# v as the stationary operand and probabilities divided before they are turned, in a two-layer attention and mixture-of-experts kernel

## What is computed

```python
q = (xn @ w_q).reshape(b, n, HEADS, DIM_HEAD).transpose(0, 2, 1, 3)
k, v = jnp.split(xn @ w_kv, 2, axis=-1)            # and the same for k and v
k = jnp.concatenate([nk, k], axis=2)               # 2 null keys in front of 256
v = jnp.concatenate([nv, v], axis=2)
sim = einsum(l2norm(q), l2norm(k)) * 8.0 + alibi, causal
out = softmax(sim) @ v
out = out.transpose(...).reshape(b, n, HEADS * DIM_HEAD) @ w_out
```

## Time and profile before

| | us |
|---|---|
| median of three timed executions | 655.25 (651.95 to 656.0) |
| the profiled execution, its own time | 660.73 |
| its span from first to last instruction | 658.9 |

### The profile page before, as it was taken

How to read it: one execution, slowest core, us unless ns; L and a number is a source line. 1 busy time by engine, 2 the same in 40 slices (tenths; PEclk the granted TensorE clock), 3 DMA queues, 4 the chain that set the end, 5 groups by cost and what they waited for, 6 DMA issues and landing times.

```text
span 658.9 us, 13422 instructions
## 1 busy us (share of the span) xinstructions
PE 573.4 (87%) x3792; PEld 453.3 (69%) x3792; DVE 421.6 (64%) x1523; ACT 430.3 (65%) x1197; POOL 356.6 (54%) x310
## 2 busy tenths in 40 slices
PE   2446979987899989888999999999999999998787
PEld 1444768875567767766777777777877777777566
DVE  5773836455688676889655665665656566577653
ACT  2712857535677787766577777767767776877562
POOL 3618845033888697444275544544455433688830
PEclk9999979999699999999999999999999999999899
DMA  9502223140110013000000000011001100111100
GB/s 317 197 4 53 70 68 74 49 152 16 27 32 25 18 33 97 1 1 2 1 24 23 25 22 23 27 29 21 21 27 29 25 14 10 29 48 49 53 21 9
DMA packets 26326, 29.13 MB, mean 44 GB/s; under 512 B 3920, under 2 KB 22384, under 8 KB 25744
## 3 DMA queue, kind: packets, MB, share of 16 engines
q1 hardware_dynamic: 21680, 18.89, 8.9%
q0 software_dynamic: 4576, 9.38, 6.2%
HBM read 19.94 MB, written 8.32 MB: 43 GB/s over the span
## 4 chain that ended last, share of the span: by engine, by line
PE 59%; DVE 15%; POOL 11%; issue 9%; ACT 3%; DMA 1%; another core or an unknown queue 1%; SPq 0%; POOLq 0%; DVEq 0%; ACTq 0%
PE b_last L1816 8%; PE b_upB L1801 7%; POOL taken L622 5%; PE b_rest L1865 4%; PE b_upB L1787 4%; PE b_last L1679 3%; POOL rn L571 3%; PE b_rest L1654 3%; PE b_rest L1613 2%; PE b_upA L1472 2%; PE b_upA L1734 2%; PE b_last L1472 2%; PE b_rest L1836 2%; PE b_upA L1474 2%; PE b_upA L1473 2%
## 5 line engine op out<-in xcount | busy, mean ns | idle before, releaser
L868 ACT ACTIVATE prb<-prb,mneg 128x130 f32<-128x130 f32 (+1 forms) x256 | 114.8, 450 | 93.9 <-DVE mneg L1415 89.4
L571 POOL TENSOR_TENSOR rn<-ss,halves 128x8 f32<-128x8 f32 x64 | 107.6, 1681 | 102.0 <-DVE ss L1353 101.3
L1415 DVE CUSTOM_DVE_ANT_0 prb<-b_upB,bias 128x130 f32<-128x130 f32 (+1 forms) x256 | 82.1, 356 | 122.1 <-PE b_upB L1801 117.5
L499 POOL DMA_INDIRECT moe_buf<-normal_rows,source x79 | 78.8, 997 | 103.1 <-PE b_rest L1768 63.5
L1816 PEld LDWEIGHTS b_last<-v,prT_all 128*128 128x128 f32 x768 | 100.0, 192 | 12.6 <-DVE qs_all L1401 4.8
L1816 PE MATMUL b_last<-v,prT_all 128*128 128x64 f32 x768 | 101.4, 268 | 3.0 <-DVE qs_all L1401 2.4
L1801 PE MATMUL b_upB<-qkT 64*128 64x258 f32 (+1 forms) x512 | 77.7, 381 | 0.0
L877 ACT ACTIVATE prT_all<-b_rest 128x512 f32<-128x512 f32 (+1 forms) x128 | 61.5, 480 | 10.9 <-PE b_rest L1865 7.8
L1865 PE MATMUL b_rest<-cst,prb 128*128 128x128 f32 x384 | 63.6, 275 | 0.0
L314 POOL TENSOR_TENSOR qk<-qk,rn 128x512 f32<-128x512 f32 x56 | 59.1, 1055 | 4.4
L1865 PEld LDWEIGHTS b_rest<-cst,prb 128*128 128x128 f32 x384 | 47.6, 150 | 18.0 <-issue 17.8
(11 more groups left out here) (325 smaller groups left out, 1294.2 us busy)
## 6 DMA issues: line engine op xcount, KB each, us to landing
expert_rows<-moe_buf SPq DMA_DIRECT2D x20, 128.0 KB
expert_rows<-moe_buf SPq DMA_DIRECT2D x39, 64.0 KB
bias<-w_up SPq DMA_DIRECT2D x1, 2048.0 KB, 8.9
down<-w_dn SPq DMA_DIRECT2D x2, 1024.0 KB, 10.0
moe_buf<-w_up SPq DMA_DIRECT2D x4, 512.0 KB, 3.9
moe_buf<-normal_rows,source POOLq DMA_INDIRECT x79
qk<-x SPq DMA_DIRECT2D x8, 128.0 KB, 4.0
v<-w_qk SPq DMA_DIRECT2D x1, 1024.0 KB, 11.5
```

What stands on the lines that cost most here:

```text
L499: nc.gpsimd.indirect_dma_start(out=room, out_offset=None, in_=normal_rows[layer], in_offset=bass.IndirectOffsetOnAxis(ap=source[layer][:, ...
L571: nc.gpsimd.tensor_tensor(rn[hs], ss[hs], halves[:], ALU.pow).then_inc(pool_root, 1)
L868: nc.scalar.activation(prb[k % 3][:, i, 0:n], prb[k % 3][:, i, 0:n], ACT.Exp, scale=-1.0, bias=mneg[:, qt, h:h + 1], accum_out=lsum[:, qt, ...
L1415: nc.vector.tensor_tensor_reduce(prb[k % 3][:, i, 0:n], b_sim[i][:, 0:n], bias[:, h, KEYS - n:KEYS], 1.0, FMAX, ALU.add, ALU.min, mneg[:, ...
```

## The change

Four things are changed together.

1. The values matmul is swapped: `v` (64 columns of one head) is stationary, `prT` (128 columns) moves. The output comes out with channels on the partitions, head 0 of a pair in partitions 0 to 63 and head 1 in 64 to 127 of `b_pv`, so the turn L1836 and the copy out of `b_y` are gone; one VectorE copy takes `b_pv` to `oT`. The built program puts these matmuls on array tiles of 128 rows by 64 columns, at column 0 for head 0 and column 64 for head 1.
2. The null values are swapped likewise: four float32r matmuls of 128 moving columns in place of one of 512.
3. Since the sums now run along the wrong axis for a division behind the matmul, the probabilities are divided while they still have a query on each partition: for every step VectorE takes two reciprocals and multiplies head 0, and head 1 is multiplied by ScalarE for k < 32 and by GpSimd from there on.
4. The division takes a turn of its own: turning, copying, null columns and values come one turn later. The first layer's row gathers on GpSimd are spread over turns.

```diff
@@ GpSimd
-                if s % 3 == 0 and 0 <= s < 3 * (B - 2):
-                    take_rows(s // 3 + 2)
+                for b in range(2, B):
+                    parts = [n for n in range(2 * T) if s == 3 * (b - 2) + 2 * n // 3]
+                    if parts:
+                        take_rows(b, parts)
...
+            def shares(s):
+                for k in [k for k in step_at(s, 1) if k >= ACT_SHARES]:
+                    qt, hp = divmod(k % STEPS, HP)
+                    n, h = NULL + P * (qt + 1), 2 * hp + 1
+                    pool.wait_ge(dve_rl, k + 1)
+                    pool.wait_ge(act_exp, 2 * k + 2)
+                    mine = prb[k % 3][:, 1, 0:n]
+                    nc.gpsimd.tensor_tensor(mine, mine, rl[:, qt, h:h + 1].to_broadcast([P, n]), ALU.mult).then_inc(pool_share, 1)
...
-            all_steps(rows, tile_rows, take_tiles, front)
+            all_steps(shares, rows, tile_rows, take_tiles, front)
@@ ScalarE
+            def shares(s):
+                for k in [k for k in step_at(s, 1) if k < ACT_SHARES]:
...
+                    nc.scalar.activation(prb[k % 3][:, 1, 0:n], prb[k % 3][:, 1, 0:n], ACT.Copy, scale=rl[:, qt, h:h + 1]).then_inc(act_share, 1)
...
-                for k in step_at(s, 1):
+                for k in step_at(s, 2):
@@ VectorE, scores(s)
-                for m in quad_at(s, 7):
...
-                    nc.vector.reciprocal(heads8, lsum[:, tile, first:first + HALF]).then_inc(dve_rl, 1)
...
-                    nc.vector.tensor_tensor(o_half[m % 2].rearrange("p (h d) -> p h d", h=HALF), b_pv.rearrange("p (h d) -> p h d", h=HALF),
-                                            heads8.unsqueeze(2).to_broadcast([P, HALF, DH1]), ALU.mult).then_inc(dve_norm, 1)
+                for m in quad_at(s, 8):
+
+                    dve.wait_ge(pe_pvn, m + 1)
+                    if m:
+                        dve.wait_ge(pe_op, m)
+                    nc.vector.tensor_copy(oT[:].rearrange("p a q -> p (a q)"), b_pv).then_inc(dve_oT, 1)
...
-                for m in quad_at(s, 5):
+                for k in step_at(s, 1):
+
+                    qt, hp = divmod(k % STEPS, HP)
+                    n, h = NULL + P * (qt + 1), 2 * hp
+                    dve.wait_ge(act_exp, 2 * k + 2)
+                    nc.vector.reciprocal(rl[:, qt, h:h + 2], lsum[:, qt, h:h + 2]).then_inc(dve_rl, 1)
+                    dve.wait_ge(dve_rl, k + 1)
+                    mine = prb[k % 3][:, 0, 0:n]
+                    nc.vector.tensor_scalar(mine, mine, rl[:, qt, h:h + 1], None, ALU.mult).then_inc(dve_share, 1)
+                for m in quad_at(s, 6):
...
-                for k in step_at(s, 1):
+                for k in step_at(s, 2):
...
-                    dve.wait_ge(act_exp, 2 * k + 2)
+                    dve.wait_ge(dve_share, k + 1)
+                    if k < ACT_SHARES:
+                        dve.wait_ge(act_share, k + 1)
+                    else:
+                        dve.wait_ge(pool_share, k + 1 - ACT_SHARES)
@@ TensorE
-                for k in step_at(s, 3):
+                for k in step_at(s, 4):
...
-                    for i in range(2):
-                        h = 2 * (p % HP) + i
-                        at = (k % 4 * 2 + i) * DH1
-                        for c in range(p // HP + 1):
-                            ins = nc.tensor.matmul(b_pv[:, at:at + DH1], prT[k % 3][:, i, c * P:(c + 1) * P], v[:, c, h * DH1:(h + 1) * DH1],
-                                                   start=(k % 4 == 0 and i == 0 and c == 0), stop=False, skip_group_check=True)
+                    at = k % 4 * P
+                    for c in range(p // HP + 1):
+                        for i in range(2):
+                            h = 2 * (p % HP) + i
+                            ins = nc.tensor.matmul(b_pv[i * DH1:(i + 1) * DH1, at:at + P], v[:, c, h * DH1:(h + 1) * DH1],
+                                                   prT[k % 3][:, i, c * P:(c + 1) * P], start=(k % 4 == 0 and c == 0), stop=False,
+                                                   skip_group_check=True)
...
-                    nc.tensor.matmul(b_pv, pnT[:], nvbd[:, m % 2], start=False, stop=True, skip_group_check=True).then_inc(pe_pvn, 1)
+                    for a in range(4):
+                        ins = nc.tensor.matmul(b_pv[:, a * P:(a + 1) * P], nvbd[:, m % 2, a * P:(a + 1) * P], pnT[:], start=False, stop=(a == 3),
+                                               skip_group_check=True)
...
-                    for i in range(4):
-                        ins = nc.tensor.transpose(b_y[:, i * P:(i + 1) * P], o_half[m % 2][:, i * P:(i + 1) * P], ident)
-                    ins.then_inc(pe_oT, 1)
...
-                    pe.wait_ge(act_exp, 2 * k + 2)
+                    pe.wait_ge(dve_share, k + 1)
+                    if k < ACT_SHARES:
+                        pe.wait_ge(act_share, k + 1)
+                    else:
+                        pe.wait_ge(pool_share, k + 1 - ACT_SHARES)
```

More of the change, by code:

```diff
@@ L159, in build @@
         qsT = [qs_all[:, i * S:(i + 1) * S] for i in range(RING)]
-        o_half = [qs_all[:, i * 512:(i + 1) * 512] for i in range(2)]
         mix = [sb(f"mix{i}", [P, D]) for i in range(2)]
@@ L297, in build @@
         pool_root, unit = sem("pool_root"), sem("unit")
-        pe_sim, pe_prT, pe_pv, pe_pnT, pe_pvn, pe_oT, pe_op = (
-            sem(f"pe_{n}") for n in ("sim", "prT", "pv", "pnT", "pvn", "oT", "op"))
-        dve_sim, dve_null, dve_pnh, dve_pnT, dve_rl, dve_norm, dve_oT, dve_add = (
-            sem(f"dve_{n}") for n in ("sim", "null", "pnh", "pnT", "rl", "norm", "oT", "add"))
+        pe_sim, pe_prT, pe_pv, pe_pnT, pe_pvn, pe_op = (
+            sem(f"pe_{n}") for n in ("sim", "prT", "pv", "pnT", "pvn", "op"))
+        dve_sim, dve_null, dve_pnh, dve_pnT, dve_rl, dve_share, dve_oT, dve_add = (
+            sem(f"dve_{n}") for n in ("sim", "null", "pnh", "pnT", "rl", "share", "oT", "add"))
+        act_share, pool_share = sem("act_share"), sem("pool_share")
         act_exp, act_prT = sem("act_exp"), sem("act_prT")
@@ L526, in _, with take_rows @@
             nc.gpsimd.tensor_tensor(nvbd[low], raw_nv[low], nvbd[low].bitcast(F32), ALU.subtract).then_inc(nv_set, 1)
-            def take_rows(b):
+            def take_rows(b, parts=range(2 * T)):
                 if b == 0:
@@ L878, in values @@
                                          ACT.Copy).then_inc(act_prT, 1)
-            all_steps(tile_parts, scores, router_inputs, route1, front, values, attention_rows, late_mixing)
+            all_steps(tile_parts, scores, shares, router_inputs, route1, front, values, attention_rows, late_mixing)
         @block.vector
@@ L1797, in scores @@
                             pe.wait_ge(dve_sim, 2 * k - 1 + i)
-                        for m in quad_at(k - 1, 10) if i else quad_at(k - 1, 5):
+                        for m in quad_at(k - 1, 10) if i else quad_at(k - 1, 6):
                             pe.wait_ge(dve_add if i else dve_pnT, m + 1)
```

47 lines of the change are left out of this document (16 added, 31 removed).

## The result

The changed kernel takes 708.47 us (median of 4 runs, 705.71 to 709.43) against 653.67 for the kernel before on the same chip: a ratio of 1.083, 95% interval 1.078 to 1.088. I had forecast 675 and a range of 643 to 706. The direction was right, the size was not: +55 us and not +20, outside the range.

A forecast was written before the change was run, and what follows sets the result against it. It took no single engine to bound before 275 us, TensorE from 333 to 566 and GpSimd from 566 to 632. Its terms, 7 + 8 - 12 - 3 - 1.5 + 12 + 2 + 8 = +20.5 on 655.25, gave 675 us, range 643 to 706.

The forecast's parts named there:

- the depth that I put at nothing: Pipeline: dividing one turn of the loop later was to cost nothing where TensorE is full.
- VectorE's +12: Tile turns: reciprocal, multiplication and port sharing add 0.8 us, 0.4 after slack, in 27 one-chunk turns; +12 us (0 to 31).
- Values matmuls, +7 us: Swapped values matmuls outside the GpSimd stretch: 56 short steps +0.18 us each, 54 long steps -0.05; +7 us.
- null values, +8: Four float32r null matmuls in place of L1824: +0.30 us in each of 27 quads, +8 us (+4 to +16).
- the output's turn, -12: L1836 leaves TensorE: 0.44 us saved in each of 27 quads, -12 us.
- rival (a): Values matmuls: the two heads do not run side by side, 36 us on top, 711 us; chance 0.12.
- my trip of 0.35: Values matmuls: changing TensorE's array shape into column halves and back was put at 0.35 us.
- The turn as a wait, -3: VectorE's 23.0 us of waiting for L1836 ahead of L1457 mostly lay beside TensorE's stream; -3 us (0 to -23).
- Rival (b): VectorE's wait for the output's turn comes back, its additions hide, null values cost loads only; 647 us, chance 0.17.
- ScalarE, +2: First 32 steps: 32 multiplications of some 0.45 us, partly in ScalarE's idle time; +2 us (0 to 14).
- GpSimd, +8: Late stretch: 16 added multiplications, 8 of 0.6 us and 8 of 0.4; +8 us (6 to 15); hidden elsewhere.
- Rival (e): Outside the late stretch GpSimd's shares arrive late, TensorE's turning waits 0.3 us in 78 turns; +20, 695 us; chance 0.08.

## Why the prediction was wrong, step by step

Two steps failed, and they meet in one turn of every quad: the depth that I put at nothing, and VectorE's +12, which I placed in the wrong turns. A third, the clock, I left out.

**"The extra turn of depth costs nothing where TensorE is full."** It moves the null columns' copies (0.28 + 0.28 us) from the quad's turn 5 to 6, the turn in which VectorE also adds the output (L1462, 0.29) and the value projection waits for the tile's subtraction. 0.989 against 0.973 prices it, without any share, at 1.6%, some 10 us (6.5 in the profiles). I had counted what the depth gives (time for the share) and not what it moves into another turn. The diff shows the copies going from 5 to 6; I looked at VectorE's order in the tile turn of the earlier trace rows alone. The projection is not what matters in it: moved a turn later, the stop stayed, at 21.6 us.

**"VectorE, +12 us."** The mechanism was right (a longer piece ahead of TensorE's tile work), the place and the size were not. I priced the ordinary tile turn, where the slack of the earlier trace rows took most of it: the waits for L1391 and L1383 there are 5.6 us. The price fell in the 12 turns with the value projection, at 1.8 us each, 21.4 us, which moving one instruction removed. My 0.8 us of addition in a turn, worked out as 0.2 + 0.3 + 0.3, were about right: 0.16 for the reciprocal, and for the multiplication 0.53 or 0.81 beside GpSimd's share (0.29 or 0.36 with GpSimd idle). The sharing of the port was put on the wrong row: the null copy's median did not rise to 0.4 us,
in the view of one line (shortest, median, longest ns, first and last start),

```profile
L1476 DVE COPY pn<-prb x128: 150/165/586, 166.2 to 696.6; 128x12 f32<-128x12 f32 x128
```

since GpSimd's share is long done by then; it is the multiplication L1441 that meets it. It ends 0.08 us (130 columns) or 0.15 us (258) after GpSimd's instruction has ended, whether that one takes 0.39, 0.61 or, as L314 does, 1.04 us: 460.76 + 0.81 against 460.81 + 0.61, and 470.05 + 0.98 against 469.83 + 1.04 in the views above. So VectorE stands until GpSimd is through. This is what the Trainium skill says of the port ("SBUF — State Buffer", section "SBUF: two separate sides"), a lock held for the whole instruction, which I had tied to the null copy; the trace agrees.

**The clock was no term at all.** The earlier trace rows show 1.00 for turns 48 to 95, and I took it as given. In the changed kernel 23.8 us of it ran at half clock, which does the work of 11.9. TensorE's busy time says the same: 207.36 against 195.80 with the subtraction moved, 11.6 us. Stops of 1.59 to 2.48 us come before it. The length of a stop alone does not decide: with all on ScalarE 12 stops of 1.12 to 2.02 us left the clock whole, with TensorE turning first one stop of 1.89 was followed by half clock, and with the projection a turn later one of 1.37 was. What else decides is not shown. So of the 31.4 us, 22.2 are TensorE standing, 11.6 the clock, and -2.4 its own work.

**Values matmuls, +7 us; null values, +8; the output's turn, -12.** The heads do run side by side: rival (a) is false. Here is TensorE with the subtraction moved, a long step and a short one (start, length):

```profile
465.18 0.66 PE L1699 MATMUL b_last<-cst,qk 128*128 128x128 f32 x4
465.76 0.66 PE L1835 MATMUL b_last<-prT_all,v 128*64 128x128 f32 x8
466.35 0.66 PE L1879 MATMUL b_rest<-cst,prb 128*128 128x128 f32 x4
466.85 0.38 PE L1764 MATMUL b_upA<-cst,th 128*128 128x128 f32 x2
...
462.56 0.44 PE L1835 MATMUL b_last<-prT_all,v 128*64 128x128 f32 x4
462.93 0.67 PE L1845 MATMUL b_last<-pnT,nvbd 96*128 96x128 f32 x4
463.43 0.63 PE L1879 MATMUL b_rest<-cst,prb 128*128 128x128 f32 x4
```

From start to start, eight records of values matmuls take 466.35 - 465.76 = 0.59 us and four 0.37: pairs pass together, 0.44 and 0.22, and 0.15 is the way out of the shape. The next block, L1879, takes 0.50, 0.06 more than its four passes, and L1699 ahead of them 0.58, 0.14 more. That sums to my trip of 0.35. But part of the way in had been paid before as well; here is the kernel before:

```profile
455.71 0.66 PE L1679 MATMUL b_last<-cst,qk 128*128 128x128 f32 x4
456.20 1.00 PE L1816 MATMUL b_last<-v,prT_all 128*128 128x64 f32 x8
```

0.49 for the same four turns, so only 0.09 of the way in is new. A long step is 0.59 + 0.06 + 0.09 - 0.84 = -0.10, a short one 0.37 + 0.15 - 0.39 = +0.13, and the term 56 x 0.13 - 54 x 0.10, about +2. The four null matmuls pass in 0.11 us each as at my floor, and their block takes 463.43 - 462.93 = 0.50, but L1824 had held the next matmul back by as much (465.35 to 465.85 in the trace before), so that my +0.30 for a quad looks too large. Read apart they can't be; together over turns 48 to 95 the swap alone has TensorE busy for 194.75 us against 198.19, -3.4, where my three terms for these 24 short and 24 long steps and 12 quads give 3.1 + 3.6 - 5.3 = +1.4.

**The turn as a wait, -3.** Too little: the swap alone is 17 us faster (ratio 0.973), where my terms without VectorE's and GpSimd's additions give -1.5. 8 us of it are in turns 0 to 47, where by the earlier trace rows no engine had much room, so that a lost multiplication, turn and wait can count directly; which of them it is was not told apart. Rival (b) had this part right, but its other half, additions that hide in VectorE's idle time, wrong.

**ScalarE, +2, and its room in turns 0 to 47.** With no division those turns are 8.3 us shorter than before, in the changed kernel 7.5 longer: the shares cost 16 us there. I had 3. In the earlier trace rows three engines are near 80% or above and VectorE at 76%, so little hides. Part of it is the clock: in turns 16 to 47 it is 0.94 in the changed kernel and 1.00 with the subtraction moved, which has the same instructions there and takes 2.8 us less.

**GpSimd, +8.** The round was right: 8.92 and 9.08 for a forecast of 8.6 to 9.0. From the first of the 32 gathers to the last it is 65.2 us for 58.6, +6.6. But this was only the part inside the rounds. The shares tie TensorE's turning to GpSimd's place in its own queue, so that no turn can run ahead of it, ahead of the gathers and behind them too: from turn 96 on the total is +17.8, and 14.6 of it go when ScalarE multiplies. Rival (e), shares that arrive late and stop the turning, happened here (waits from 590 to 657 us):

```profile
DVE pn L1476 <- POOL prb L603: 14.5, 6, 3.7
...
PE b_rest L1879 <- POOL prb L603: 12.1, 5, 3.3
```

I had put it in the stretch where GpSimd has room (0.3 us in each of 78 turns, which is 23 and not the 20 that I added), and there it is 0.3 us in all.

**The last quad, -1.5**, is small beside the rest: from turn 127 to the end it is 13.4 us for 13.0, and only without the depth 11.7.

**What is not settled**: why the loop starts 10 us later on three of the chips; what, beside the length of a stop, makes the clock fall; and how often it falls in runs that were not profiled (in the four of the changed kernel its mean is between 0.937 and 0.956).

## What to carry to other kernels

Don't count a pipeline that gets a turn deeper as free: list what moves to another turn with it, and look at each engine's list in *that* turn, above all at the instruction behind which another engine waits. Before pricing an operation by its length, ask what stands behind it in its engine's order; here one short subtraction, placed ahead of the new work, was worth 4.5% of the kernel before's time. And an operation given to an engine that lags behind in its own queue ties everyone who reads the result to that lag. GpSimd's multiplications show it: from turn 96 on, where GpSimd was the bound, they cost 14.6 us more than on ScalarE, and in the first 32 steps 29 us more.

## What was not expected of the hardware

TensorE's clock, at full level for all of turns 48 to 95 before, fell to half for 3.4 us behind seven of twelve stops of 1.38 to 2.48 us: each of the seven cost 1.7 us on top of itself. Two matmuls with 64 stationary columns each, on the two column halves, pass 128 moving columns each in the time of one. VectorE's multiplication, released together with GpSimd's by the same reciprocal, starts 0.05 us ahead of it in the trace and still ends 0.08 or 0.15 us behind it: 0.53 and 0.81 us for 0.29 and 0.36.
